# Filler matmuls on two 64-row halves of the array, one item apart, behind both score pairs of an odd step; the residual tile replaced in halves

## The chip, the cores and the metric

The kernel runs on one core of a Trainium2 chip. Its engines are TensorE (PE in the profile, its weight loads PEld), VectorE (DVE), ScalarE (ACT), GpSimd (POOL) and SyncE (SP), which issues the DMAs. The metric is the time of one launch on the device, in microseconds.

## The reference

One transformer layer on x of 16 batches x 1024 tokens x 256, in float32, with 16 heads of 16:

```python
q, k, v = (split_heads(x @ W.T + b) for W, b in ((Wq, bq), (Wk, bk), (Wv, bv)))
attn = softmax(einsum('hbnd,hbmd->hbnm', k, q) * (1 / 16), axis=-1)
out = merge_heads(einsum('hbnm,hbmd->hbnd', attn, v)) @ Wo.T + bo
x = layernorm(x + out)
h = silu(x @ w_gate.T / 127) * (x @ w_up.T / 127)      # 768 wide
x = layernorm(x + h @ w_down.T / 127)
```

## The kernel before

**Steps.** A batch is 64 steps: 4 groups of 4 heads, two halves of 512 tokens, 8 tiles of 128 (k in 0..63). In each step the function score does two pairs of heads, pair 0 and pair 1. A pair is two matmuls that lie on partitions 0 to 50 and 64 to 114, so on the two 64-row halves of the array, side by side. Their result goes to scores[pair], two banks of PSUM; ACT makes the exponentials from it (L608) into probs. There are only the two pairs of banks, so pair p of step k+1 waits until the exponential of pair p of step k is done (probs_ready). The function products multiplies probs with v for two steps at once, at every even step, for steps k-2 and k-1: 16 float32 matmuls, each on all 128 rows and 32 columns of the array, four side by side.

**Fillers.** Everything else that PE has to do is cut into items and put between the steps: of the next batch qk (8 items of 6 matmuls of 512 columns), norm (2) and v (4 items of 12 matmuls of 256 columns); of the batch before out (4 of 12), x1T (4 items of 4 float32 transposes of 128), gate and up (12 each, 4 matmuls of 512) and down (4 items of 24 matmuls of 256). Apart from norm they use all 128 rows and 128 columns. FULL_BLOCKS gives the items of the 32 visits, one at each odd step: qk, out and x1T in the first 10, one gate and one up in each of the next 12, v and down in the last 10. An item takes one of the three ring banks (RINGS = 3) and, at its start, waits on ring_free for the item three before it to be drained. The drain is DVE's (drain_item), for qk and gate with an ACT instruction ahead of it (hi L580, tanh L589).

**Order on the engines.** All engines run in program order. On PE an odd step is pair 0, pair 1, fillers; an even step is pair 0, pair 1, products of two steps. Plan gives the orders of DVE, ACT and POOL from due times that are written out by hand. In a middle batch (1 to 14) they are FULL_PLAN's. Batch 0 has only the items of the next batch, batch 15 only those of the one before.

**The residual.** x_res, 1 MB, holds the residual and later the result. At the end of a batch SP stores the result in two halves, waits for both, loads the whole of the next x (L447 and near), and POOL adds the bias to all of it in one instruction (add_bias, L530); out 0 is drained after that.

**Names in the prediction.** take and scale are DVE's take_segment and scale_segment, which bring the sums of a finished half group from PSUM and divide; xT is scale_x (x to two float16 parts in x16, L799 and L801); x1 and y are normalise (L822), which waits for POOL's rstd (L510).

Of the kernel before, what the change touches and what calls it, by code (L numbers as in the profile page):

```python
# [9 lines left out]
ALU = mybir.AluOpType  # L10
# [4 lines left out]
P = 128  # L15
BATCHES = 16
TOKENS = 1024
DIM = 256
# [44 lines left out]
STACK = ROWS + SHIFT_ROWS  # L63

# [9 lines left out]
        "gate": (4, 216), "up": (4, 216), "down": (24, 108)}  # L74
PRE, POST = ("qk", "norm", "v"), ("out", "x1T", "gate", "up", "down")
# [10 lines left out]
def evenly(items, steps):  # L86
# [4 lines left out]
    for kind, j in items:  # L91
# [3 lines left out]
        for m in sorted(set(where)):  # L95
# [3 lines left out]
FULL_BLOCKS = (evenly(some("qk", 0, 1, 2, 3) + some("out", 0, 1, 2, 3)  # L99
                      + [item for j in range(4) for item in some("x1T", j) + some("qk", 4 + j)], 20)  # L100
               + [some("norm", *{3: (0,), 5: (1,)}.get(g, ())) + gate_up(g) for g in range(2 * HCHUNKS)]
               + evenly(some("v", 0, 1) + some("down", 0) + some("v", 2, 3) + some("down", 1, 2, 3), 20))
FULL = list(dict.fromkeys((kind, j) for block in FULL_BLOCKS for kind, j, *_ in block))

# [9 lines left out]
ONLY_POST = [item for item in FULL if item[0] in POST]  # L114
# [4 lines left out]
def base(b):  # L119

    return len(FIRST) if isinstance(b, int) and b == 0 else len(FIRST) + len(ONLY_PRE) + len(FULL) * (b - 1)


PREPARE = 8
XMAX, SCALE = 6, 22
POOL_XMAX, POOL_NORMS = 12.2, 48.9
# [66 lines left out]

PREPARES = [PER_GROUP * g + PREPARE for g in range(GROUPS - 1)] + [STEPS - 6]
FULL_PLAN, PRE_PLAN, POST_PLAN = Plan(FULL_BLOCKS, PREPARES), Plan(evenly(ONLY_PRE, PRE_STEPS), PREPARES), Plan(POST_BLOCKS, PREPARES[:-1])
# [7 lines left out]
def build(nc, x, xt, Wq_t, bq, Wk_t, bk, Wv_t, bv, Wo_t, bo, gate_t, up_t, down_t, out):  # L203
    ctx = ExitStack()
    with ctx:  # L205
# [113 lines left out]
        x_pre_loaded, x_res_loaded, x_res_biased = sem("x_pre_loaded"), sem("x_res_loaded"), sem("x_res_biased")  # L319
        ring_fill, ring_free = sem("ring_fill"), sem("ring_free")  # L320
# [20 lines left out]
        def _(sp):  # L341
# [32 lines left out]
            def store_result(b):  # L374
                for s in range(2):

                    sp.wait_ge(y_ready, 4 * b + 2 * (s + 1))
                    sp.dma_start(out_v[b][:, TPH * s:TPH * (s + 1), :], x_res[:, TPH * s:TPH * (s + 1), :]
                                 ).then_inc(out_stored, 16)


# [14 lines left out]
            def batch(b, first, last, ahead=2):  # L396
                if first:
                    load_stack(b, 1)
# [4 lines left out]
                if not first:  # L403
                    sp.wait_ge(scores_ready, UNITS * b)
                    load_stack(b, 1)
# [895 lines left out]
```

## Time and profile before

| | us |
|---|---|
| median of 3 runs | 2544.46 |
| lowest, highest | 2544.41, 2547.49 |
| span of the profiled execution | 2544.0 |
| PE busy in it | 2470.4 (97%) |
| ACT busy in it | 2132.0 (84%) |
| DVE busy in it | 1399.0 (55%) |
| POOL busy in it | 539.6 (21%) |

The busy time of PE is not that of a full array: the ends of matmuls are modelled, and a row with four matmuls of a pair of heads counts from the first start to the last end. What the array does is read from the starts: the time from the start of one group of matmuls to the start of the next.

### The profile page before, as it was taken

The numbers are of one execution on the slowest core, as the hardware profiler recorded it, in microseconds if no ns is written. First come the engines' busy times: TensorE is split into PE (matmuls) and PEld (weight loads), VectorE is DVE, ScalarE is ACT, GpSimd is POOL, SyncE is SP. The second block draws the span as 40 slices with busy tenths as digits, with TensorE's granted clock in tenths as the row PEclk, the third lists the DMA queues.
The fourth block names the chain that finished last, engine by engine and source line by source line (L and its number), as shares of the span: only waits on it lengthen the run. The fifth ranks groups of instructions, "written<-read, shape, count | busy, mean of one in ns | idle before, by whom it ended". The sixth has DMA issues, their size and how long they took to land. (4 is left out here: it accounts for less than half of the span.)

```text
span 2544.0 us, 48910 instructions
## 1 busy us (share of the span) xinstructions
PE 2470.4 (97%) x18062; PEld 884.2 (35%) x18062; DVE 1399.0 (55%) x3008; ACT 2132.0 (84%) x2370; POOL 539.6 (21%) x542
## 2 busy tenths in 40 slices
PE   4999999999999999999999999999999999999996
PEld 2223343433324333343433324333343433333333
DVE  5334556464654655556564654646465565654547
ACT  1997888888888888888888888888889888898881
POOL 2102222131221212222131221212222131221113
PEclk8999999999999999999999999999999999999998
DMA  4112021030212103021021202103121120212000
GB/s 145 50 49 79 28 88 43 23 101 27 91 33 75 59 17 109 23 85 43 31 93 27 93 31 81 55 15 109 27 81 43 37 87 26 93 31 60 27 22 29
DMA packets 81750, 144.20 MB, mean 57 GB/s; under 512 B 27584, under 2 KB 29504, under 8 KB 79424
## 3 DMA queue, kind: packets, MB, share of 16 engines
q1 hardware_dynamic: 79968, 139.81, 17.4%
q8 instruction: 178, 2.92, 0.5%
q14 instruction: 100, 0.82, 0.1%
q10 hardware_dynamic: 1504, 0.66, 0.1%
HBM read 88.48 MB, written 50.33 MB: 55 GB/s over the span
## 5 line engine op out<-in xcount | busy, mean ns | idle before, releaser
L608 ACT ACTIVATE probs<-psum 128x1024 f32<-128x1024 f32 x2048 | 1984.8, 1024 | 312.5 <-PE psum L1045 311.8
L1045 PE MATMUL psum<-probs,v 128*32 128x512 f32 x8192 | 995.7, 600 | 0.9 <-DVE flipped L877 0.4
L1045 PE MATMUL psum<-kstack,qstack 51*128 51x512 f16 x4096 | 637.5, 383 | 18.7 <-ACT probs L608 10.4
L1045 PEld LDWEIGHTS psum<-kstack,qstack 51*128 51x128 f16 x4096 | 150.5, 93 | 679.9 <-ACT probs L608 596.5
L1045 PEld LDWEIGHTS psum<-probs,v 128*32 128x32 f32 x8192 | 211.2, 109 | 470.3 <-issue 468.1
L517 POOL TENSOR_TENSOR ffn<-h,ffn 128x512 f16<-128x512 f32 x192 | 222.0, 1156 | 675.8 <-DVE ffn L793 675.8
L747 DVE SCALAR_TENSOR_TENSOR tanh_out<-tanh_out,psum 128x512 f32<-128x512 f32 x192 | 131.6, 686 | 287.2 <-ACT tanh_out L589 287.2
L510 POOL TENSOR_TENSOR rstd<-vareps,minus_half 128x2 f32<-128x2 f32 x128 | 91.1, 712 | 720.9 <-DVE vareps L815 720.8
L738 DVE SCALAR_TENSOR_TENSOR parts<-psum,scales,parts 128x512 f16<-128x512 f32 x128 | 95.3, 745 | 199.5 <-ACT parts L580 199.4
L1045 PE MATMUL psum<-ffn,gateT 128*128 128x512 f16 x768 | 199.8, 383 | 0.3 <-DVE ffn L781 0.3
L1045 PE MATMUL psum<-ffn,upT 128*128 128x512 f16 x768 | 198.0, 380 | 0.4
L1045 PE MATMUL psum<-downT,ffn 128*128 128x256 bf16 x1536 | 188.5, 273 | 0.0
L877 DVE STREAM_TRANSPOSE flipped<-psum 128x512 f32<-128x512 f32 x128 | 91.6, 716 | 170.3 <-PE psum L1045 170.3
L496 POOL TENSOR_TENSOR squares<-parts 128x512 bf16<-128x512 f16 x128 | 130.9, 1046 | 225.2 <-DVE parts L738 167.3
L1045 PEld LDWEIGHTS psum<-downT,ffn 128*128 128x128 f16 x1536 | 141.5, 98 | 59.6 <-issue 44.3
L789 DVE SCALAR_TENSOR_TENSOR h<-tanh_out,h_scale,psum 128x512 f32<-128x512 f32 x192 | 143.5, 747 | 18.7 <-DVE tanh_out L747 0.5
L589 ACT ACTIVATE tanh_out<-psum 128x512 f32<-128x512 f32 x192 | 116.3, 606 | 42.3 <-PE psum L1045 42.3
L822 DVE TENSOR_SCALAR x_res<-x_res,meanvar,rstd 128x256 f32<-128x256 f32 x256 | 93.4, 407 | 67.0 <-POOL rstd L510 67.0
L773 DVE SCALAR_TENSOR_TENSOR x_res<-psum,down_scale,x_res 128x512 f32<-128x512 f32 x64 | 47.9, 749 | 138.9 <-PE psum L1045 138.9
L580 ACT ACTIVATE parts<-psum,scales 128x512 f16<-128x512 f32 x128 | 88.9, 696 | 31.8 <-PE psum L1045 24.3
L530 POOL TENSOR_TENSOR x_res<-x_res,bo_all 128x2048 f32<-128x2048 f32 x16 | 72.6, 4540 | 169.5 <-DMA x_res<-in_L_attn_x 169.5
L1045 PEld LDWEIGHTS psum<-ffn,upT 128*128 128x128 bf16 x768 | 74.6, 98 | 93.9 <-DVE tanh_out L747 4.9
(120 smaller groups left out, 1617.0 us busy)
## 6 DMA issues: line engine op xcount, KB each, us to landing
parts_dram<-parts SPq DMA_DIRECT2D x64, 512.0 KB, 2.9
qstack<-parts_dram SPq DMA_DIRECT2D x384, 64.0 KB, 2.1
kstack<-parts_dram SPq DMA_DIRECT2D x384, 64.0 KB, 2.2
x_pre<-in_x_t SPq DMA_DIRECT2D x17, 1024.0 KB, 7.3
x_res<-in_L_attn_x SPq DMA_DIRECT2D x16, 1024.0 KB, 4.8
out<-x_res SPq DMA_DIRECT2D x32, 512.0 KB, 2.7
kstack<-shift_parts SPq DMA_DIRECT2D x384, 4.0 KB, 1.7
ffn<-in_L_ffn_w_gate SPq DMA_DIRECT2D x1, 768.0 KB, 7.1
```

The source lines that it names most:

```text
L496: nc.gpsimd.tensor_tensor(squares[:, idx, cols], parts[:, idx % 2, 0, cols], parts[:, idx % 2, 0, cols], ALU.mult).then_inc(squares_ready, 1)
L510: nc.gpsimd.tensor_tensor(rstd[:, tiles], vareps[:, tiles], minus_half[:, tiles], ALU.pow).then_inc(rstd_ready, 1)
L517: nc.gpsimd.tensor_tensor(hT[hf][1][:, hc, :], h32[:, g % 2, :], hT[hf][0][:, hc, :], ALU.subtract).then_inc(h_lo_ready, 1)
L580: nc.scalar.activation(parts[:, idx % 2, 0, hf * HALF:(hf + 1) * HALF], bank[RING + (start + n) % RINGS], ACT.Identity, bias=scales[:, par ...
L589: nc.scalar.activation(tanh_out[:, g % 2, :], bank[RING + (start + n) % RINGS], ACT.Tanh, scale=0.5 * W_SCALE).then_inc(tanh_ready, 1)
L608: nc.scalar.activation(probs[:, (STEPS * b + k) % SLOTS, 2 * pr:2 * pr + 2, :], scores[pr], ACT.Exp, scale=score_scale[par]).then_inc(prob ...
L738: nc.vector.scalar_tensor_tensor(out=parts[:, idx % 2, 1, cols], in0=o, scalar=scale[:, BIAS + idx:BIAS + idx + 1], in1=parts[:, idx % 2, ...
L747: nc.vector.scalar_tensor_tensor(out=gated, in0=gated, scalar=1.0, in1=o, op0=ALU.add, op1=ALU.mult).then_inc(ring_free, 1)
L789: nc.vector.scalar_tensor_tensor(out=h32[:, j % 2, :], in0=tanh_out[:, j % 2, :], scalar=h_scale[:, 0:1], in1=o, op0=ALU.mult, op1=ALU.mul ...
L822: ins = nc.vector.tensor_scalar(x_res[:, t, :], x_res[:, t, :], meanvar[:, t, 0:1], rstd[:, t:t + 1], ALU.subtract, ALU.mult)
L877: nc.vector.transpose(flipped[:, hf, :], bank[ACC]).then_inc(acc_free, 1)
L1045: return nc.tensor.matmul(o, lhsT, rhs, start=start, stop=stop)
```

## The change

Fillers of the middle batches are done on half the rows. MAIN lists the items in order: out 0 to 3, qk 0 to 7, gate and up 0 to 11, tile 0 to 7 (down, cut to one token tile each), v 0 to 3. Each item is done twice over the same columns: first its matmuls on partitions 0 to 63 (LOW), and then those on 64 to 127 (HIGH) into the same bank. A slot holds the LOW matmuls of one item and the HIGH matmuls of the item before it, one by the other: 1 + 1 of 512 columns, or 2 + 2 of 256. The first HIGH matmul of an item waits on the new semaphore half_made for the end of the last LOW matmul of that item. out, qk, tile and v have 6 slots, gate and up 4. The last item (v 3) is carried: its HIGH half comes in the next batch. VISITS gives 242 slots to the 32 odd steps, all behind both pairs. x1T and norm are done whole, on all rows, as side items: at even steps 8, 10, 12, 14 and 26, 30, between the pairs and the products. A new class Rolled gives the orders of DVE, ACT and POOL. Since v 3 needs the old x16, xT is now done at the start of the next batch, behind v 3 and ahead of the drain of out 0; the search for the maximum of x starts at step 9 in place of 6. x_res is stored, loaded and given its bias in two halves, each with its own semaphore.

```diff
+LOW, HIGH = slice(0, ROW_TILE), slice(ROW_TILE, P)
+MAIN = (some("out", 0, 1, 2, 3) + some("qk", *range(8)) + gate_up(*range(2 * HCHUNKS)) + some("tile", *range(TILES))
+        + some("v", 0, 1, 2, 3))
+CARRY = MAIN[-1]
+WIDTH = {"out": 6, "qk": 6, "gate": 4, "up": 4, "tile": 6, "v": 6}
+VISITS = [(0, count, 0) for count in (
+    8, 8, 8, 6, 6, 6, 6, 9, 9, 10, 6, 10, 6, 10, 6, 10, 8, 8, 8, 8, 8, 8, 7, 7, 8, 6, 8, 7, 7, 8, 6, 6)]
+SIDES = {3: ("x1T", 0), 4: ("x1T", 1), 5: ("x1T", 2), 6: ("x1T", 3), 12: ("norm", 0), 14: ("norm", 1)}
-XMAX, SCALE = 6, 22
-POOL_XMAX, POOL_NORMS = 12.2, 48.9
+XMAX, SCALE = 9, 22
+POOL_XMAX, POOL_NORMS = 14.2, 48.9
...
+class Rolled(Plan):
+    def __init__(self, prepares, carried, carries):
+        slots = []
+        for phase in range(len(MAIN) + (not carries)):
+            low = phase if phase < len(MAIN) else None
+            high = phase - 1 if phase or carried else None
+            wide = [0 if n is None else WIDTH[MAIN[n][0]] for n in (low, high)]
+            slots += [(low if i < wide[0] else None, high if i < wide[1] else None, i) for i in range(max(wide))]
...
+        if carried:
+            last = carry_ready
+            dve = [(last, "v", CARRY[1], -1)] + [(last + 0.3 + 1.5 * hf, "xT", hf, 0) for hf in range(HALVES)]
...
+            def replace_half(b, s):
+                store_half(b, s)
+                sp.wait_ge(out_stored, 32 * b + 16 * (s + 1))
+                sp.dma_start(x_res[:, TPH * s:TPH * (s + 1), :], x_v[1:BATCHES][b][:, TPH * s:TPH * (s + 1), :]
+                             ).then_inc(x_res_loaded[s], 16)
...
-                    store_result(b - 1)
-
-                    sp.wait_ge(out_stored, 32 * b)
-                    sp.dma_start(x_res[:, :, :], x_v[1:BATCHES][b - 1]).then_inc(x_res_loaded, 16)
+                    replace_half(b - 1, 0)
+                    load_shift(b + 1, 0)
+                    replace_half(b - 1, 1)
...
+            def half_waits(plan, kind, j, n, start, pre, post):
+                pe.wait_ge(ring_free, start + n - RINGS + 1)
...
+            def slot(plan, b, low, high, i, w_parts):
+                todo = []
+                for rows, which in ((LOW, low), (HIGH, high)):
+                    if which is not None:
+                        kind, j = MAIN[which]
+                        each = COST[kind][0] // WIDTH[kind]
+                        todo += [(m / each, rows, which, kind, j, each * i + m) for m in range(each)]
+                for _, rows, which, kind, j, m in sorted(todo, key=lambda entry: entry[0]):
+                    n = plan.number(which)
+                    if m == 0 and rows is LOW:
+                        half_waits(plan, kind, j, n, base(b), b + 1, b - 1)
+                    elif m == 0:
+                        pe.wait_ge(half_made, len(MAIN) * (b - 1) + which + 1)
+                    ins = half_mm(kind, j, m, rows, bank[RING + (base(b) + n) % RINGS], w_parts)
+                    if m == COST[kind][0] - 1:
+                        ins.then_inc(half_made if rows is LOW else ring_fill, 1)
...
+            def full(b, par, w_parts):
+                plan = plan_of(b)
+                for k in range(STEPS):
...
+                    here = plan.segments[(k - 1) // 2] if k else ((), (), ())
+                    score(b, k, False, (0,))
...
+                    for low, high, i in here[0 if k % 2 else 2]:
+                        slot(plan, b, low, high, i, w_parts)
+                    score(b, k, False, (1,))
+                    if k % 2:
+                        for low, high, i in here[1]:
+                            slot(plan, b, low, high, i, w_parts)
+                        continue
+                    if k and k // 2 - 1 in SIDES:
+                        n = plan.place(*SIDES[k // 2 - 1])
+                        do_item(plan, n, 0, COST[plan.items[n][0]][0], base(b), b + 1, b - 1, w_parts)
+                    for earlier in (k - 2, k - 1):
...
             def everything(w_parts):
                 for b in range(1, BATCHES - 1, 2):
-                    batch(b, 1, False, False, w_parts)
-                    batch(b + 1, 0, False, False, w_parts)
+                    full(b, 1, w_parts)
+                    full(b + 1, 0, w_parts)
```

## Rows read from the trace of the kernel before

**Rows 1.** The page's first part: busy time of each engine, its share and instructions.

```profile
PE 2470.4 (97%) x18062; PEld 884.2 (35%) x18062; DVE 1399.0 (55%) x3008; ACT 2132.0 (84%) x2370; POOL 539.6 (21%) x542
```

**Rows 2.** One middle batch: its length, busy time (count) PE, PEld, DVE, ACT, POOL; clock.

```profile
1265.48:1417.52 152.04, 152.04 (x1129) 54.94 (x1129) 85.44 (x184) 133.12 (x149) 33.20 (x33) 1.00 0.18 57
```

**Rows 3.** Timeline of PE (start, us, engine, line, operation, count), gate and up visit.

```profile
1202.51 0.61 PE L1045 MATMUL psum<-kstack,qstack 51*128 51x512 f16 x4
1203.05 1.04 PE L1045 MATMUL psum<-ffn,gateT 128*128 128x512 f16 x4
1203.92 1.03 PE L1045 MATMUL psum<-ffn,upT 128*128 128x512 f16 x4
1204.88 0.61 PE L1045 MATMUL psum<-kstack,qstack 51*128 51x512 f16 x4
1205.42 1.92 PE L1045 MATMUL psum<-probs,v 128*32 128x512 f32 x16
```

**Rows 4.** Timeline of all engines, the same visit: ACT, tanh and two exponentials.

```profile
1204.77 0.60 ACT L589 ACTIVATE tanh_out<-psum 128x512 f32<-128x512 f32 x1
1205.31 1.94 ACT L608 ACTIVATE probs<-psum 128x1024 f32<-128x1024 f32 x2
```

**Rows 5.** Timeline of all engines, PE in a short visit of 14 down matmuls.

```profile
1263.31 0.61 PE L1045 MATMUL psum<-kstack,qstack 51*128 51x512 f16 x4
1263.84 1.70 PE L1045 MATMUL psum<-downT,ffn 128*128 128x256 bf16 x14
1265.48 0.64 PE L1045 MATMUL psum<-kstack,qstack 51*128 51x512 f16 x4
1266.05 1.92 PE L1045 MATMUL psum<-probs,v 128*32 128x512 f32 x16
1267.91 0.61 PE L1045 MATMUL psum<-kstack,qstack 51*128 51x512 f16 x4
```

**Rows 6.** Timeline of PE: an x1T item ahead of qk, a norm ahead of gate.

```profile
1297.08 0.66 PE L1048 MATMUL psum<-ident,x_res 128*128 128x128 f32 x4
1297.57 1.46 PE L1045 MATMUL psum<-x,Wq 128*128 128x512 f16 x6
...
1330.62 0.40 PE L1045 MATMUL psum<-squares,heads 128*32 128x512 bf16 x4
1330.95 1.04 PE L1045 MATMUL psum<-ffn,gateT 128*128 128x512 f16 x4
```

**Rows 7.** Timeline of DVE: scale, the drain of out, x1, x1T, xT.

```profile
1270.00 0.25 DVE L885 RECIPROCAL inv<-flipped 128x16 f32<-128x16 f32 x1
...
1272.12 0.69 DVE L896 TENSOR_TENSOR out<-flipped,out 128x512 f16<-128x512 f32 x1
...
1290.83 0.74 DVE L768 SCALAR_TENSOR_TENSOR x_res<-psum,out_scale,x_res 128x512 f32<-128x512 f32 x1
...
1293.79 0.74 DVE L822 TENSOR_SCALAR x_res<-x_res,meanvar,rstd 128x256 f32<-128x256 f32 x2 [0.80 <-POOL rstd L510]
...
1302.61 0.68 DVE L779 CAST ffn<-psum 128x512 f16<-128x512 f32 x1
1303.37 0.69 DVE L781 TENSOR_TENSOR ffn<-psum,ffn 128x512 f16<-128x512 f32 x1
...
1397.07 0.75 DVE L799 TENSOR_SCALAR x<-x_pre,scales 128x1024 f16<-128x1024 f32 x1
1397.89 1.28 DVE L801 SCALAR_TENSOR_TENSOR x<-x_pre,scales,x 128x1024 f16<-128x1024 f32 x1
```

**Rows 8.** Timeline of ACT: hi of a qk item, behind the exponentials.

```profile
1274.92 0.70 ACT L580 ACTIVATE parts<-psum,scales 128x512 f16<-128x512 f32 x1
```

**Rows 9.** Timeline of POOL: the bias added to all of x_res.

```profile
1277.31 4.54 POOL L530 TENSOR_TENSOR x_res<-x_res,bo_all 128x2048 f32<-128x2048 f32 x1 [8.79 <-DMA x_res<-in_L_attn_x]
```

**Rows 10.** The page's DMA issues: count, KB of one, us from issue to landing.

```profile
x_res<-in_L_attn_x SPq DMA_DIRECT2D x16, 1024.0 KB, 4.8
out<-x_res SPq DMA_DIRECT2D x32, 512.0 KB, 2.7
```

More of the change, by code:

```diff
@@ L73 @@
 COST = {"x1T": (4, 109), "qk": (6, 216), "norm": (1, 330), "v": (12, 108), "out": (12, 108),
-        "gate": (4, 216), "up": (4, 216), "down": (24, 108)}
-PRE, POST = ("qk", "norm", "v"), ("out", "x1T", "gate", "up", "down")
+        "gate": (4, 216), "up": (4, 216), "down": (24, 108), "tile": (12, 108)}
 def some(kind, *js):
@@ L113 @@
                + [half for j in range(4) for half in halves("down", j)])
-ONLY_POST = [item for item in FULL if item[0] in POST]
+ONLY_POST = (some("out", 0, 1, 2, 3) + some("x1T", 0, 1, 2, 3) + gate_up(*range(2 * HCHUNKS)) + some("down", 0, 1, 2, 3))
 FIRST = some("qk", *range(QK)) + some("v", 0) + some("norm", 0, 1) + some("v", 1, 2, 3)
@@ L396, in batch @@
             def batch(b, first, last, ahead=2):
-                if first:
-                    load_stack(b, 1)
+                if not first:
+                    sp.wait_ge(scores_ready, UNITS * b)
+                load_stack(b, 1)
                 if not last:
@@ L451, in _ @@
             batch(BATCHES - 1, False, True)
-            store_result(BATCHES - 1)
+            for s in range(2):
+                store_half(BATCHES - 1, s)
             sp.wait_ge(out_stored, 32 * BATCHES)
@@ L592, in batch @@
             def batch(b, par, first, last):
[L593 removed]
+                plan = plan_of(b, first, last)
                 def extras(k, h):
@@ L775, in drain_item @@
                     find_stats(j)
+                elif kind == "tile":
+                    nc.vector.scalar_tensor_tensor(out=x_res[:, j, :], in0=o[:, 0:DIM], scalar=down_scale[:, 0:1],
+                                                   in1=x_res[:, j, :], op0=ALU.mult, op1=ALU.add).then_inc(ring_free, 1)
+                    if j % 2:
+                        find_stats(j // 2)
                 elif kind == "x1T":
@@ L899, in batch @@
             def batch(b, par, first, last):
-                plan = PRE_PLAN if first else POST_PLAN if last else FULL_PLAN
+                plan = plan_of(b, first, last)
                 def once(k):
@@ L1146, in do_item @@
                     ins.then_inc(ring_fill, 1)
+            def half_waits(plan, kind, j, n, start, pre, post):
+                pe.wait_ge(ring_free, start + n - RINGS + 1)
+                if kind == "qk" and j < 2:
+                    pe.wait_ge(x_scaled, 2 * pre + j + 1)
+                elif kind == "out" and j % 2 == 0:
+                    pe.wait_ge(out_ready, 4 * post + 3 + j // 2)
+                elif kind == "gate":
+                    if j == 0 and post == 0:
+                        pe.wait_ge(ffn_weights_ready, 1)
+                    if j % HCHUNKS == 0:
+                        pe.wait_ge(ring_free, start + plan.place("x1T", 2 * (j // HCHUNKS) + 1) + 1)
+                elif kind == "tile" and j % TPH == 0:
+                    pe.wait_ge(h_lo_ready, 2 * HCHUNKS * post + HCHUNKS * (j // TPH + 1))
```

178 lines of the change are left out of this document (143 added, 35 removed).

## The prediction

> **What bounds the kernel now.** First the page's busy times: PE 97%, ACT 84%, DVE 55% [rows 1]; the reader is to see that only PE and ACT can be the bound. Then the length of one middle batch by stretch: 152.04 us at full clock, ACT busy 133 of them [rows 2]. There are 14 such batches, 2129 of the 2544.0 us; only they are changed much. Then the timeline of PE. A visit with gate and up, from pair 0 of an odd step: 0.54 us to the fillers, 1.83 to the next pair, 0.54 to the products [rows 3], 1.86 to the pair after them [rows 5], in sum 4.77. Nothing waits in it. One round of 512 columns takes 0.216 (gate to up 0.87 for four, 0.01 of it for the first) [rows 3]. So two rounds of scores leave 0.11 of the 0.54, and eight filler rounds leave 0.10 of the 1.83: **about 0.10 is lost each time the array goes from one tiling to another**, four times per visit.
>
> But ACT is close behind. In a short visit (14 x 0.109 us of fillers), PE's second pair row lasts 0.64 in place of 0.61: it waits for ACT [rows 5]. From the odd step's pair 0 to the products 2.74 pass, and with the products (1.86) the visit takes 4.60 [rows 5]. The 2.74 is a chain, not PE's work: 0.43 from pair 0 to its exponential, 1.94 for two exponentials [rows 4], 0.05 back, 0.31 from pair 1 to the products. Since the products stand behind pair 1 of the even step, which needs the odd step's second exponential, **no visit can be shorter than 4.60**, however few fillers it has.
>
> **The change, part by part.**
>
> *Two tiling changes fewer.* Scores and fillers are now both on 64-row halves. A visit of c slots then takes on PE 0.44 (two pairs) + 0.216c + 0.54 + 1.86. With c = 8 that is 4.57, so the floor of 4.60 holds: 0.17 less than 4.77, not the 0.20 removed. With 9 it is 4.78, with 10 5.00, with 6 or 7 the floor, 4.60. The Trainium skill, "TensorEngine Tiling (Array Packing)", section Tiling Modes, says that changing the mode drains the array; the 0.10 of rows 3 is that, and no more than that is to be won.
>
> *Half matmuls.* The rows of the scores show two halves side by side: four matmuls of 512 columns in 0.43 [rows 3]. So I take a slot at 0.216, whole items' price; 242 slots against 240 before, since two boundaries between items of 4 and of 6 slots leave a half idle. Twice the weight loads are at no cost if they run side by side as the scores' do.
>
> *The new wait.* At the first HIGH matmul of an item PE waits for the end of the LOW half of the same item, which it issued one round earlier. Behind it in PE's queue stands everything, first the next LOW matmul. No row shows PE waiting for itself. The nearest: ACT starts 0.43 after the start of the pair that it reads [rows 4]. A round of 0.216 lies between, so HIGH starts 0.21 behind LOW. It keeps that lag, and pair 0 of the even step, with ACT and the products behind it, comes as much later. A second boundary in the same visit costs nothing more, as HIGH's own lane is by then as late. Bounds: 0 if the wait is answered at once (nothing can be gained by it), 0.27 if PE is as slow as after other engines. I take 0.20. It falls in the 25 visits with a boundary behind their first slot; the other seven (visits 3 to 6, 25, 30, 31, counted from 0) have 6 slots. So c = 8 gives 4.77, 9 gives 4.98, 10 gives 5.20; in a visit of 7 (2.69 to the products against 2.74) or 6 the floor hides it.
>
> *Sum over the visits.* VISITS has 8 twelve times, 9 twice, 10 four times, 7 four times, 6 ten times: 12 x 4.77 + 2 x 4.98 + 4 x 5.20 + 14 x 4.60 = 152.4.
>
> *Side items.* An x1T took 0.49 inside the fillers [rows 6]. Between pair 1 and the products it adds a tiling change, 0.59, in a visit of 6 that already waits for ACT in its odd step; the two do not overlap, since x1T stands behind the wait. Four: 2.4. A norm has the tiling of the products: 0.22 for one round, in place of 0.33 [rows 6]; two: 0.4. Together 2.8.
>
> *hi and tanh.* They stand behind the odd step's second exponential. One of 0.6 (tanh [rows 4]) or 0.7 (hi [rows 8]) just fits into ACT's pause of the even step; two in one visit (visit 8, visit 10) don't, and pair 1 of the next odd step waits some 0.5. I take 1.0 in all.
>
> *xT at the head of the batch.* DVE's queue there, from when the last products of the batch before are done, 2.5 us in: take 0.6, scale 2.8 and a pause to 6.1, v 3 to 6.7, xT twice 2.1 to 10.9, out 0 with its statistics 2.1 (from its start to x1's, less the pause of 0.80), 0.8 for POOL's rstd, x1 0.65, out 1 and out 2 to 18.6 (out 2's bank free at 17.3), x1 twice, out 3 to 22.2, x1T 0 1.45 to 23.6 [rows 7]. PE comes to qk 0 (odd step 7) at 3 x 4.77 + 2.8 = 17.1 and waits 0.2 for out 2's bank; to qk 1 (step 9) at 22.3 and waits 1.4 for x1T 0's, of which 0.45 would have been spent on ACT anyway. Net 1.2. Unhidden it was 0 before, as xT lay in a stretch where DVE waited. Bounds 0.3 and 3; I take 1.0.
>
> *Ring.* A bank is now held for two phases, so gate g+1 waits for the drain of up g-1 one phase earlier. In an 8-slot visit this falls together with the lag above; in three of the 10-slot visits it may add 0.2 each. Taken at nothing, 0.6 in the range.
>
> *Residual in halves, and SP.* The whole bias took 4.54 and began 12 us into the batch [rows 9]. Now y 3 is due at step 60, so about 10 us before the batch's end; store and load (2.7 and at most 4.8 [rows 10]) and a half's bias of 2.3 end near its start, and out 0 is drained 10.9 in. Cost 0. On SP the halves' waits stand ahead of the next stack and shift loads; these are due at the next batch's step 0 (shift, moved ahead of the second half) and step 16, so several us off: 0. If that cover failed, PE would wait once per batch for about one load of 2 to 5.
>
> *Total.* 152.4 + 2.8 + 1.0 + 1.0 = 157.2 per batch against 152.04: +5.1, times 14 is +71. Against the profiled execution's 2544.0 (the median of the runs is 0.5 more): **2615**.
>
> **Rivals.**
>
> *The wait is answered at once* (no lag; for it: nothing in the trace shows the wait). Then 12 x 4.60 + 2 x 4.78 + 4 x 5.00 + 14 x 4.60 = 149.2, with the same 4.8 behind it 154.0: +2.0 a batch, 2572.
>
> *Faster: PE's own work sets the time.* The mechanism is that ACT's chain shifts against PE's from visit to visit, so that short visits are not held at the floor and the 10,6,10,6 pattern averages out. With no lag, a batch is 32 x 2.84 + 242 x 0.216 + 2.8 = 146.0, plus 1 to 2 for DVE: -4.5 to -5, 2480. It decides where a visit of 6 slots takes under 4.5. Against it: the 4.60 of rows 5. For it: PE's 97% [rows 1]. A mixture of this and the last (some lag, some averaging) gives about 2544, no change.
>
> *PE is short of instructions.* Half matmuls double the filler instructions; of 256 columns they come at one per 54 ns, with a weight load each. The fastest fillers now are one matmul and one load per 0.109 [rows 5]. If that were the limit, the 96 slots of out, tile and v would take 0.44: up to +20 a batch; if a tenth of that, 2645. The Trainium skill, "TensorE: Matmul & The Clock Gate", section "Wait — 56ns, not 53.3ns?", gives about 62 ns per matmul where the sequencer decodes them in software; by that such a slot is estimated at 0.25 and the sum at some 40 us more, in place of nothing. No row here shows a rate above one per 0.109 kept up.
>
> *The halves don't run side by side.* A slot would cost 0.43, over 3200. The scores speak against it.
>
> **How the numbers follow.** Forecast 0.46; answered at once 0.16; PE alone, faster 0.25; mixture, no change 0.07; short of instructions 0.05; halves one after the other 0.01. Its own range: lag 0.15 to 0.27 and DVE 0.3 to 3 give 2585 to 2660. The range reaches down into the faster case: 2495 to 2665. Faster by over 0.2% (what a measurement can tell) 0.25, within 0.2% 0.07, slower 0.68.
>
> **What would show it.** In the profile after: pair to fillers 0.43 to 0.45 and fillers to pair without the 0.10 (step one). HIGH's first matmul of an item 0.2 behind LOW's, and the even step's pairs late by as much (the lag). Visits of 6 slots at 4.60, with x1T at 5.2, visits of 10 at 5.2 (the floor). PE waiting on DVE at steps 7 and 9, DVE without a pause from 3 to 24 us in. The prediction is wrong if 6-slot visits are shorter than 4.5, if 8-slot gate visits take 4.6, or if slots of 256 columns take more than 0.22.

## The result and the profile after

| | before | after |
|---|---|---|
| median of the runs, us | 2544.43 (4 runs: 2542.72 to 2547.49) | 2797.73 (4 runs: 2789.18 to 2799.03) |
| ratio, 95% interval | | 1.0987 [1.097, 1.1005] |
| span of the profiled execution, us | 2544.0 | 2786.8 |
| mean granted clock of PE in it | 0.990 | 0.973 |

The kernel became 253 us slower; the forecast was 71 slower. Parts 1 and 2 of the page of the changed kernel: busy time of each engine, and PE's busy tenths and granted clock in 40 slices.

```profile
PE 2539.2 (91%) x22766; PEld 947.6 (34%) x22766; DVE 1442.5 (52%) x3060; ACT 2142.5 (77%) x2370; POOL 546.1 (20%) x558
...
PE   4988998989999898998989989899899998989997
...
PEclk9999999999999999999999999999999999999998
```

Against [rows 1], every engine's share fell, PE's from 97% to 91%, although PE's busy time rose by 69 us. So PE stands still, and not for want of an engine with more work: the new time is waiting. The table of waits of the changed kernel says for what (waiting engine and line, releaser: us in total, times, longest):

```profile
PEld psum L1160 <- ACT probs L715: 599.7, 801, 3.1
...
PEld psum L1160 <- DVE h L901: 154.7, 165, 3.9
...
PE psum L1160 <- DVE h L901: 97.0, 56, 3.4
...
PEld psum L1160 <- PE psum L1160: 87.9, 305, 0.3
...
ACT parts L687 <- DMA parts_dram<-parts: 45.3, 15, 7.5
```

The first line, the waits of the scores for the exponentials, is what it was before (598.7). L901 is DVE's drain of an up item, and behind it is 3.9 us at the longest. In the kernel before, the same pair of lines stands at 0.4:

```profile
PEld psum L1045 <- DVE h L789: 12.1, 39, 0.4
```

Next, where in a batch the time is lost. The table gives the length of each visit (from the start of the first products matmul of an even step to that of the next; median over the 14 middle batches), worked out from the starts of PE's matmuls. "Foreseen" is the prediction's own figure for that visit. Visits that are not shown agree with it within 0.03.

| visit: odd step | slots | before | foreseen | after |
|---|---|---|---|---|
| 0 to 2: 1, 3, 5 | 8 | 4.76 | 4.77 | 4.80 |
| 3, 4: 7, 9 | 6, x1T | 4.78 | 5.19 + the DVE wait | 6.16, 6.20 |
| 5, 6: 11, 13 | 6, x1T | 4.78, 4.81 | 5.19 | 5.19 |
| 7, 8: 15, 17 | 9 | 4.81 | 4.98 | 5.00 |
| 9: 19 | 10 | 4.81 | 5.20 | 5.41 |
| 10: 21 | 6 | 4.76 | 4.60 | 6.18 |
| 11: 23 | 10 | 4.76 | 5.20 | 5.74 |
| 12: 25 | 6, norm | 4.76 | 4.82 | 9.39 |
| 13: 27 | 10 | 5.09 | 5.20 | 6.35 |
| 14: 29 | 6, norm | 4.76 | 4.82 | 5.40 |
| 15: 31 | 10 | 5.09 | 5.20 | 5.20 |
| 16: 33 | 8 | 4.76 | 4.77 | 8.14 |
| 17: 35 | 8 | 4.76 | 4.77 | 5.43 |
| 20: 41 | 8 | 4.76 | 4.77 | 5.24 |
| 24, 26, 29: 49, 53, 59 | 8 | 4.60 | 4.77 | 4.80 |
| 25, 30, 31: 51, 61, 63 | 6 | 4.60 to 4.67 | 4.60 | 4.60 |

A mean middle batch takes 170.1 us against 152.2, so 14 of them are 251 of the 253. Of the 12.9 above the foreseen 157.2, visits 12 to 20 hold 10.8, of which 7.9 are in two visits, at steps 25 and 33. The rest is 1.6 at step 21 and 1.0 at steps 7 and 9 (2.0 above their 5.19, of which 1.0 was foreseen).

The timeline of PE and DVE at step 25 of one middle batch of the changed kernel (start, us, engine, line, operation; in brackets the idle time before it and its releaser):

```profile
1280.42 0.61 PE L1160 MATMUL psum<-kstack,qstack 51*128 51x512 f16 x4
1280.56 0.72 DVE L989 STREAM_TRANSPOSE flipped<-psum 128x512 f32<-128x512 f32 x1 [1.26 <-PE psum L1160]
...
1280.87 0.38 PE L1160 MATMUL psum<-ffn,gateT 64*128 64x512 f16 x1
...
1280.87 0.38 PE L1160 MATMUL psum<-ffn,upT 64*128 64x512 f16 x1
...
1281.09 0.37 PE L1160 MATMUL psum<-ffn,upT 64*128 64x512 f16 x1
...
1281.70 0.43 DVE L999 TENSOR_TENSOR scaled<-flipped,inv 128x256 f32<-128x256 f32 x1
1282.20 0.71 DVE L1004 STREAM_TRANSPOSE flipped<-scaled 128x512 f32<-128x512 f32 x1
...
1283.49 0.69 DVE L1008 TENSOR_TENSOR out<-flipped,out 128x512 f16<-128x512 f32 x1
1284.10 0.74 DVE L901 SCALAR_TENSOR_TENSOR h<-tanh_out,h_scale,psum 128x512 f32<-128x512 f32 x1
...
1284.89 0.39 PE L1160 MATMUL psum<-ffn,upT 64*128 64x512 f16 x1 [3.43 <-DVE h L901]
```

Two slots into the visit, the LOW half of up 2 wants its bank. That is the bank of up 1, whose HIGH half ended in the slot just before, at 1281.09 plus a round. Its drain L901 is ready to run, but DVE does take and scale first (from L989 at 1280.56 to L1008, done at 1284.1), since that is the order written out for it. PE starts again 0.79 after the start of the drain, 3.80 after the start of its last matmul. ACT needs no more of this time than the two exponentials of the visit, and the next scores stand behind the fillers, so nothing makes up for it.

This order came with the change. In the kernel before, up 1 is finished in the visit of step 23, and its drain stands ahead of take and scale; in the changed kernel up 1 is finished two slots into step 25, and Rolled puts it behind them. The timeline of DVE in the kernel before, at the same place of a batch (the drain of up 1, the first instruction of take, the last of scale):

```profile
1172.20 0.75 DVE L789 SCALAR_TENSOR_TENSOR h<-tanh_out,h_scale,psum 128x512 f32<-128x512 f32 x1
...
1173.41 0.72 DVE L877 STREAM_TRANSPOSE flipped<-psum 128x512 f32<-128x512 f32 x1
...
1176.53 0.69 DVE L896 TENSOR_TENSOR out<-flipped,out 128x512 f16<-128x512 f32 x1
```

The granted clock after it, in the table of stretches of the changed kernel (length, busy time (count) of PE, PEld, DVE, ACT and POOL, clock, DMA share, GB/s): from the pairs of step 24 to those of step 26, with the stall in it, and from there to the pairs of step 28, in batch 6 and then in batch 7.

```profile
1106.37:1114.97 8.60, 5.17 (x40) 1.50 (x36) 5.22 (x11) 4.29 (x5) 2.31 (x2) 0.86 0.03 6
1114.97:1122.46 7.49, 7.49 (x50) 2.13 (x48) 2.53 (x4) 4.56 (x6) 0.01 (x1) 0.71 0.00 0
1277.98:1285.77 7.79, 4.36 (x40) 1.31 (x37) 5.21 (x11) 4.28 (x5) 1.50 (x2) 1.00 0.03 5
1285.77:1291.13 5.36, 5.36 (x50) 1.92 (x48) 2.45 (x4) 4.56 (x6) 0.82 (x1) 1.00 0.01 3
```

The same 50 entries of PE take 7.49 in batch 6 and 5.36 in batch 7. In batch 6 the mean granted clock is 0.71, a mixture of the 2.4 GHz level and the 1.2 GHz one, and PE is busy all through; in batch 7 it is 1.00. PE stood still for 3.43 in the stretch ahead of it in both (8.60 less 5.17, 7.79 less 4.36). The Trainium skill, "TensorE: Matmul & The Clock Gate", section "Part 1: The HAM clock gate", says that the array's clock is halved according to how busy PE has lately been; the row of batch 6 agrees, at 2.1 us more, and that of batch 7 shows that such a stall does not always bring it. Batches 5 and 7 have a granted clock of 1.00 from end to end. In them the visits at steps 25 and 33 take 7.95 and 7.30 against the medians of 9.39 and 8.14, and the visits at steps 25 to 41 lie 6.8 above what was foreseen, where the mean of all 14 batches is 10.2. So of the 10.8, 6.8 is waiting and some 4 the half clock behind it.

### The profile page after: what moved, and what is told of

Read it like the earlier page. It is cut to its first block and busy times, and to the rows that moved or that the text cites. A ratio compares the mean times of both kernels' runs of the same rounds, so it can differ in the third digit from the quotient of the medians.

```text
span 2786.8 us, 58468 instructions
## 1 busy us (share of the span) xinstructions
PE 2539.2 (91%) x22766; PEld 947.6 (34%) x22766; DVE 1442.5 (52%) x3060; ACT 2142.5 (77%) x2370; POOL 546.1 (20%) x558
## 5 line engine op out<-in xcount | busy, mean ns | idle before, releaser
L1160 PE MATMUL psum<-kstack,qstack 51*128 51x512 f16 x4096 | 698.6, 387 | 67.7 <-ACT probs L715 57.4
L1160 PE MATMUL psum<-ffn,upT 64*128 64x512 f16 (+1 forms) x1440 | 385.6, 388 | 60.7 <-DVE h L901 60.2
L1160 PEld LDWEIGHTS psum<-kstack,qstack 51*128 51x128 f16 x4096 | 198.1, 95 | 685.1 <-ACT probs L715 584.4
L1160 PE MATMUL psum<-ffn,gateT 64*128 64x512 f16 (+1 forms) x1440 | 385.4, 389 | 37.0 <-DVE h L901 36.7
L901 DVE SCALAR_TENSOR_TENSOR h<-tanh_out,h_scale,psum 128x512 f32<-128x512 f32 x192 | 143.3, 746 | 312.2 <-PE psum L1160 309.9
L845 DVE SCALAR_TENSOR_TENSOR parts<-psum,scales,parts 128x512 f16<-128x512 f32 x128 | 94.5, 748 | 286.1 <-ACT parts L687 286.1
L1160 PE MATMUL psum<-downT,ffn 64*128 64x256 bf16 (+1 forms) x2880 | 226.7, 270 | 0.0
L989 DVE STREAM_TRANSPOSE flipped<-psum 128x512 f32<-128x512 f32 x128 | 90.6, 708 | 197.9 <-PE psum L1160 197.9
L1160 PEld LDWEIGHTS psum<-ffn,gateT 64*128 64x128 bf16 (+1 forms) x1440 | 119.1, 96 | 208.1 <-DVE h L901 76.6
L934 DVE TENSOR_SCALAR x_res<-x_res,meanvar,rstd 128x256 f32<-128x256 f32 x256 | 123.6, 524 | 120.5 <-POOL rstd L615 120.3
L1160 PEld LDWEIGHTS psum<-downT,ffn 64*128 64x128 f16 (+1 forms) x2880 | 162.7, 94 | 65.5 <-PE psum L1160 19.0
L1160 PE MATMUL psum<-x,Wq 64*128 64x512 f16 (+1 forms) x720 | 140.5, 381 | 35.8 <-DVE ffn L893 16.8
L1160 PEld LDWEIGHTS psum<-ffn,upT 64*128 64x128 bf16 (+1 forms) x1440 | 115.2, 96 | 118.4 <-DVE h L901 74.0
L687 ACT ACTIVATE parts<-psum,scales 128x512 f16<-128x512 f32 x128 | 87.2, 695 | 83.3 <-DMA parts_dram<-parts 45.3
```

Of the source, the lines that this page charges most:

```text
L687: nc.scalar.activation(parts[:, idx % 2, 0, hf * HALF:(hf + 1) * HALF], bank[RING + (start + n) % RINGS], ACT.Identity, bias=scales[:, par ...
L845: nc.vector.scalar_tensor_tensor(out=parts[:, idx % 2, 1, cols], in0=o, scalar=scale[:, BIAS + idx:BIAS + idx + 1], in1=parts[:, idx % 2, ...
L901: nc.vector.scalar_tensor_tensor(out=h32[:, j % 2, :], in0=tanh_out[:, j % 2, :], scalar=h_scale[:, 0:1], in1=o, op0=ALU.mult, op1=ALU.mul ...
L934: ins = nc.vector.tensor_scalar(x_res[:, t, :], x_res[:, t, :], meanvar[:, t, 0:1], rstd[:, t:t + 1], ALU.subtract, ALU.mult)
L989: nc.vector.transpose(flipped[:, hf, :], bank[ACC]).then_inc(acc_free, 1)
L1160: return nc.tensor.matmul(o, lhsT, rhs, start=start, stop=stop)
```

## The experiments

The theory after the result (A): two things meet. An item on two half arrays holds its bank for two phases, so the next user asks for it one phase after it was filled in place of two; behind a norm, which takes a number in the ring, it asks in the slot right behind (up 2 at step 25). And DVE's order puts the 2.8 us of scale ahead of the drain in three odd half groups (steps 25, 33, 41). The rival (B): the half matmuls, or their waits on one another, make the stalls, and DVE's line is only the last name in the list. Later a second pair: which of the two things is enough alone.

**e1: only DVE's order.** take and scale of those three half groups are due later, behind the drain of the up item.

```diff
-            dve += [(TILES * seg + 1.0, "take", seg - 1, 0), (TILES * seg + 1.4, "scale", seg - 1, 0)]
+            late = 0.49 if seg in (3, 4, 5) else 0.0
+            dve += [(TILES * seg + 1.0 + late, "take", seg - 1, 0), (TILES * seg + 1.4 + late, "scale", seg - 1, 0)]
```

> One edit to the changed kernel: in the gate stretch (segments before steps 24, 32 and 40) DVE's take and scale of the finished segment come behind the drain of up 1, up 5 and up 9, not ahead of it (due times 0.49 of a step later). Theory A (a bank is held for two phases, so the next LOW half needs the drain of an up that has just ended, and that drain stands behind 3.5 us of scale work in DVE's queue): the visit at step 25 falls from 7.8 to 8.6 us to about 5.7 (the bare drain of up 1, 1.0, is still waited for), the one at step 33 from 7.7 to 4.8, step 41 from 5.3 to 4.8, and the visits after them lose their half-clock part; some 9 us a batch, 125 in all: about 2670. Theory B (half matmuls, their loads or the lag cost the time): under 20 us less, above 2770.

Measured: 2696.05, ratio 1.060 [1.0581, 1.0619], clock 0.991. Steps 25 and 33 fell from 9.39 and 8.14 to 5.40 and 5.00, step 27 to 6.01; a batch takes 163.2. So 102 of the 253 us hang on the place of two operations in DVE's queue, those of the half clock included. It is 26 us above what was expected. Step 25 came out under the 5.7 foreseen, but part of the wait moved to the visits behind: in batches without the half clock steps 27 and 35 went from 5.20 and 4.80 to 6.01 and 5.52. Steps 33 and 41 take 5.00 in place of 4.8.

**e2: also the search for the maximum of x later on POOL.** In the changed kernel one line of ACT waits for a DMA, 15 times, 45.3 us in all and 7.5 at the longest. The timeline of DVE, POOL and ACT before step 21:

```profile
1250.38 0.75 DVE L845 SCALAR_TENSOR_TENSOR parts<-psum,scales,parts 128x512 f16<-128x512 f32 x1 [2.24 <-ACT parts L687]
...
1255.24 0.38 POOL L593 PARTITION_ALL_REDUCE xmax_all<-xmax_safe  x1 [6.82 <-issue]
...
1262.74 4.03 POOL L601 TENSOR_TENSOR squares<-parts 128x512 bf16<-128x512 f16 x4 [7.13 <-DVE parts L845]
...
1268.11 0.69 ACT L687 ACTIVATE parts<-psum,scales 128x512 f16<-128x512 f32 x1 [3.16 <-DMA parts_dram<-parts]
```

The all-reduce over the partitions shows 0.38 busy, but 6.82 us of POOL's queue go by ahead of it and another 7.13 behind it, before the squares. The profile puts the second gap on DVE's L845; but the parts that the first of these squares reads were written by 1251.13, over 11 us earlier, so it is not that wait. In e2, where the all-reduce stands elsewhere in POOL's queue, the same two gaps are 6.38 and 6.99, both put on "issue". The squares behind it come late, with them the store of parts, and with the store ACT's hi, which writes parts again; ACT's exponentials stand behind hi.

```diff
-POOL_XMAX, POOL_NORMS = 14.2, 48.9
+POOL_XMAX, POOL_NORMS = 17.2, 48.9
```

> The edit of e1_up_first, and POOL's all-reduce of the maximum of x comes behind the squares of qk 2 and qk 3 (POOL_XMAX 17.2 in place of 14.2), so that the second store of parts, for which ACT's hi of qk 6 waits, goes out earlier. Theory A2 (ACT's 3 us wait for that store holds back the exponentials at step 21): the visits at steps 21 and 23 fall from 5.9 and 6.2 to about 5.1 and 5.4, 20 us less than e1_up_first, about 2650. Rival (that wait is hidden, the visits are long by their 10 slots alone): no change from e1_up_first.

Measured: 2670.51, 1.050 [1.0481, 1.0519], 25.5 under e1 where 20 were expected. Step 21 fell from 6.21 to 4.60, the floor, and ACT's wait went from 15 times to once:

```profile
PEld psum L1161 <- DVE h L902: 76.5, 165, 1.4
...
ACT parts L688 <- DMA parts_dram<-parts: 7.6, 1, 7.6
```

The same rows show that 1.4 at the longest are still waited for the up drain (L902 here).

**d1 and d2: whole items in place of halves.** Both make an item whole (one matmul on all rows) in the slots in which its HIGH half was. The order of everything else stays. d1 still takes the bank a phase before, where the LOW half took it; d2 takes it when the item begins. The diff is the main part of d1's (do_item also gets a branch for whole tiles); d2 also drops the half_waits, since do_item has the same wait at its own first matmul.

```diff
                 for _, rows, which, kind, j, m in sorted(todo, key=lambda entry: entry[0]):
                     n = plan.number(which)
                     if m == 0 and rows is LOW:
                         half_waits(plan, kind, j, n, base(b), b + 1, b - 1)
-                    elif m == 0:
-                        pe.wait_ge(half_made, len(MAIN) * (b - 1) + which + 1)
-                    ins = half_mm(kind, j, m, rows, bank[RING + (base(b) + n) % RINGS], w_parts)
-                    if m == COST[kind][0] - 1:
-                        ins.then_inc(half_made if rows is LOW else ring_fill, 1)
+                    if rows is HIGH:
+                        do_item(plan, n, m, m + 1, base(b), b + 1, b - 1, w_parts)
```

> The changed kernel with whole matmuls: the LOW half issues only its waits (ring_free and the data), and the item is then done on all 128 rows where its HIGH half stood. Order of all engines, slots and the time for which a bank is held are those of the changed kernel; there is no half_made wait, no half matmul, and two tiling changes more in each visit. Theory A (order and banks are the cause): the long visits stay, other 8-slot visits go from 4.80 to 4.77, in all 2760 to 2810. Theory B (halves are the cause): under 2640.

> As d1_whole_early, but the waits stand where the whole item starts, so a bank is held for one phase. Theory A: against d1 each wait for a bank ends up to one phase (0.86 us of gate or up, 1.3 of qk) earlier: the stalls of 1.0 and 1.3 at steps 7 and 9 go, those of 3.8 and 2.8 at steps 25 and 33 become 2.9 and 1.9: 4 to 5 us a batch, some 60 less than d1, 2700 to 2750. If holding the bank matters little and only DVE's order does: within 20 of d1.

Measured: d1 2801.66, 1.101 [1.099, 1.103]; d2 2628.68, 1.034 [1.0322, 1.0359]. Waits for the up drain in d1:

```profile
PEld psum L1160 <- DVE h L901: 175.4, 165, 3.8
...
PE psum L1160 <- DVE h L901: 98.5, 56, 3.3
```

and in d2:

```profile
PEld psum L1160 <- DVE h L901: 3.2, 11, 0.4
```

d1 settles A against B: it has no half matmul and no half_made, has the changed kernel's waits for the up drain to the count (165 and 56), and takes as long. What the halves do to the time is in the moment at which they ask for the bank. d2 was 71 us under the lower end of what was expected. I had allowed for the stalls to become shorter by a phase of 4 slots, 0.9; but where a phase ends at a visit's end, a phase later is a visit later, so nothing of them was left (step 25 4.83, step 33 4.76).

**b1, b2, b3: the two causes put into the kernel before.** b1 puts take and scale ahead of the drain of up, b2 has each gate and up of the middle batches ask for its bank one item early (tight is true there), b3 does both.

```diff
+            ahead = blocks is FULL_BLOCKS and s in (3, 4, 5)
+            dve += [(TILES * s + (0.3 if ahead else 0.55), "take", s - 1, 0),
+                    (TILES * s + (0.4 if ahead else 1.3 if s else 2.7), "scale", s - 1, 0)]
...
-                    pe.wait_ge(ring_free, start + n - RINGS + 1)
+                    early = 2 if tight and kind in ("gate", "up") and n else 1
+                    pe.wait_ge(ring_free, start + n - RINGS + early)
```

> The kernel before with one edit, in its middle batches: DVE's take and scale of the segments that end at steps 24, 32 and 40 come ahead of the drains of up 1, up 5 and up 9. A bank is still held for one phase only. Theory A (late drains cost only where the bank is wanted at once): the drain of up 1 ends some 4 us into the fillers of step 25, its bank is wanted at step 27, so nothing waits: within 0.2% of 2544. Rival (DVE's order alone makes the stalls): three stalls of 1 to 3 us a batch, 2600 to 2650.

> The kernel before, with each gate and up of the middle batches waiting for one item more to be drained (the item two before it, not three), which is what holding a bank for two phases asks. DVE's order is that of before. Theory A: up g-1 is drained about 1.1 us after the end of its visit and wanted 3.9 after it: within 0.2% of 2544. Rival (two banks are too few in themselves): over 2600.

> Both edits on the kernel before. Theory A (only the two together cost): up 2, 0.9 us into the fillers of step 25, waits for up 1, whose drain ends 4.0 in behind take (0.7) and scale (2.8): 3.1 us, the same at step 33, 1.1 at step 41, 7.3 a batch, 102 in all, and a little for the clock behind them: 2645 to 2680. Rival (the stalls of the changed kernel need its halves or its slots): as b1 and b2, 2544.

| | us | ratio, 95% interval |
|---|---|---|
| b1, order | 2547.83 | 1.0018 [1.0009, 1.0028] |
| b2, bank | 2544.55 | 1.0005 [0.9995, 1.0014] |
| b3, both | 2697.51 | 1.0621 [1.0591, 1.065] |

Each alone costs next to nothing (b1 some 4 us, in the visit at step 27), both together 154 us. The timeline of b3, in a kernel with whole items only:

```profile
1070.15 1.04 PE L1047 MATMUL psum<-ffn,gateT 128*128 128x512 f16 x4
...
1070.88 0.42 DVE L889 TENSOR_TENSOR scaled<-flipped,inv 128x256 f32<-128x256 f32 x1
...
1073.28 0.74 DVE L791 SCALAR_TENSOR_TENSOR h<-tanh_out,h_scale,psum 128x512 f32<-128x512 f32 x1
...
1074.08 1.89 PE L1047 MATMUL psum<-ffn,upT 128*128 128x512 f16 x4 [2.89 <-DVE h L791]
```

It is the picture of the changed kernel: scaled, then the drain, and PE released by it 0.80 after its start. b3's visits at steps 25 and 33 take 9.08 and 9.11. It cost 18 us more than the top of what was expected. In batches 1, 2 and 4 the granted clock is 1.00 in the visit at step 25, and it takes 7.82 or 7.83, so 3.1 above the 4.76 of before, as foreseen; what lies above that goes with the half clock (0.969 in the mean). It shows in the rows above: the four matmuls of up take 1.89, those of gate before the stall 1.04. A stretch of it right behind the stall (columns as above):

```profile
1075.90:1081.64 5.74, 5.74 (x37) 1.40 (x37) 1.87 (x3) 4.21 (x5) 1.17 (x1) 0.87 0.03 4
```

**e3: HIGH one slot further behind LOW** from tile 1 on, against the wait of PE for itself. One slot of only HIGH is added in the last visit.

```diff
+            lows, highs = [(a, i) for a, _, i, _ in slots[head:]], [(c, i) for _, c, _, i in slots[head:]]
+            slots[head:] = [(a, c, i, m) for (a, i), (c, m) in zip(lows + [(None, 0)], [(None, 0)] + highs)]
```

> e2_up_xmax, and from tile 1 to v 3 each HIGH half starts one slot later (one slot without HIGH at the head of that stretch, one without LOW at its end, 243 slots), so that the LOW half for whose end it waits was issued two rounds earlier. Theory L (the 0.2 us by which an 8-slot visit exceeds 4.60 is PE's wait for its own LOW half): the 8-slot visits at steps 49, 53 and 59 fall by 0.2, the one at step 49 from 4.82 to about 4.60; visits of 6 and 7 slots stay, as ACT's chain holds them; 0.6 a batch, about 2662. Rival (the 0.2 is the price of running halves with 256 columns, or of twice the loads): step 49 stays at 4.8.

Measured: 2673.59, 1.0505 [1.0488, 1.0523], a batch 161.8 against e2's 161.5. The visits that the edit was for did what was expected: steps 49 and 59 went from 4.80 to 4.60. PE's timeline in such a visit of e2, and then of e3:

```profile
1293.68 0.61 PE L1161 MATMUL psum<-kstack,qstack 51*128 51x512 f16 x4
1294.13 2.14 PE L1161 MATMUL psum<-downT,ffn 64*128 64x256 bf16 x32
1296.00 0.70 PE L1161 MATMUL psum<-kstack,qstack 51*128 51x512 f16 x4
1296.63 0.64 PE L1161 MATMUL psum<-probs,v 128*32 128x512 f32 x4
```

```profile
1295.63 0.61 PE L1169 MATMUL psum<-kstack,qstack 51*128 51x512 f16 x4
1296.07 1.92 PE L1169 MATMUL psum<-downT,ffn 64*128 64x256 bf16 x32
1297.82 0.62 PE L1169 MATMUL psum<-kstack,qstack 51*128 51x512 f16 x4
1298.37 1.06 PE L1169 MATMUL psum<-probs,v 128*32 128x512 f32 x8
```

In both, pair to fillers is 0.45 and 0.44; fillers to the next pair is 1.87 with the wait and 1.75 without, and the products follow 0.63 and 0.55 behind it. The lag of one round is what a visit of 8 pays above the floor. It is lost again at step 7, which went from 6.10 to 6.57, and step 53 stayed at 4.79. The traces say where. At step 53 PE waits at its first filler for the bank of a tile, so for DVE again. At the head, POOL's bias of the second half of x_res starts 2.43 us behind the first products of the batch in e3 and 1.96 in e2 (medians of batches 2 to 14), and the DVE instruction that runs beside it lasts until it is done; step 7 grows by the same 0.47. The timeline of e3 at step 53 and, of the same batch, at its head, where a CAST of 0.43 takes 2.55:

```profile
1305.42 0.66 PEld L1169 LDWEIGHTS psum<-downT,ffn 64*128 64x128 f16 x14 [0.48 <-DVE x_res L893]
```

```profile
1173.11 2.37 POOL L646 TENSOR_TENSOR x_res<-x_res,bo_all 128x1024 f32<-128x1024 f32 x1 [9.97 <-DMA x_res<-in_L_attn_x]
1173.21 2.55 DVE L1015 CAST out<-flipped 128x512 f16<-128x512 f32 x1
```

**e4 and e5: even visits.** e4 takes the 10,6 pattern away (8 slots in all 13 visits from step 19 on), moves the norms to visits 13 and 17, and has scale (but not take) behind the drain; it keeps e2's place of the all-reduce and has 7 slots in place of 6 at steps 51 and 61. e5 is e4 with d2's whole items, asked for late.

```diff
-    8, 8, 8, 6, 6, 6, 6, 9, 9, 10, 6, 10, 6, 10, 6, 10, 8, 8, 8, 8, 8, 8, 7, 7, 8, 6, 8, 7, 7, 8, 6, 6)]
+    8, 8, 8, 6, 6, 6, 6, 9, 9, 8, 8, 8, 8, 8, 8, 8, 8, 8, 8, 8, 8, 8, 7, 7, 8, 7, 8, 7, 7, 8, 7, 6)]
-SIDES = {3: ("x1T", 0), 4: ("x1T", 1), 5: ("x1T", 2), 6: ("x1T", 3), 12: ("norm", 0), 14: ("norm", 1)}
+SIDES = {3: ("x1T", 0), 4: ("x1T", 1), 5: ("x1T", 2), 6: ("x1T", 3), 13: ("norm", 0), 17: ("norm", 1)}
```

> The changed kernel with POOL_XMAX 17.2, the slots spread evenly over the gate stretch (8 in each visit from step 19 on in place of 10 and 6 in turn, one gate and one up in each, 7 in place of 6 at steps 51 and 61), the norms at steps 28 and 36, away from the segments, and DVE's scale (not its take) behind up 1, up 5 and up 9. Theory F (a short visit costs 4.60 whatever it holds, so unequal visits lose what the long ones add; and a norm makes the next LOW half need an up that has just ended): the 13 visits from step 19 to 43 take 64 to 65 in place of 67.9 in e2_up_xmax, 3 less a batch, about 2630. Rival (time goes by the number of slots alone): no change from e2_up_xmax, 2670.

> e4_even with whole matmuls on 128 rows in place of the two halves, and the waits where the whole item starts (a bank is held for one phase, four tiling changes in a visit, no half_made). Theory A: what is left of the waits for banks goes (steps 7 and 9, and behind the norms, 3 to 4 us a batch), while 8-slot visits stay at 4.77: about 2580. Theory B (the halves' two tiling changes fewer are worth their 0.2 once the order is right): slower than e4_even.

Measured: e4 2665.76, 1.0481 [1.0464, 1.0499], so 5 us better than e2 where 40 were expected. Its 13 even visits sum to 66.7 against 67.7: the two with a norm take 6.58 each, the others 4.60 to 5.28. Outside them step 7 rose from 6.10 to 6.51 and step 53 from 4.80 to 5.22. A norm takes a number in the ring, and the item behind it is thereby set against a bank filled one item later; with halves that costs the wait for a drain in both places tried (in e4 PE stands for 1.54 at steps 27 and 35, released by L901). e5 came to 2582.78, 1.0154 [1.0137, 1.0171], as expected: there the same two visits take 4.99. Its wait for the up drain:

```profile
PEld psum L1160 <- DVE h L901: 3.2, 11, 0.4
```

So of the 121 us that e4 has above the kernel before, 83 go when the bank is asked for late and the halves (with their lag) are gone. The 38 that stay lie mostly in visits 3 to 9, at the head of the batch and in the x1T as side items: step 7 takes 5.93 in e5, steps 9 to 13 5.19, against 4.8 before. The kernel before remains the fastest of all that ran.

**e6: less xT at the head of the batch.** As e2, with the second xT instruction cut to 32 of its columns; this leaves out most of the low float16 part of x.

```diff
+                    nc.vector.scalar_tensor_tensor(out=x16[:, 1, 0, hf * HALF:hf * HALF + 32],
+                                                   in0=x_pre[:, 0, hf * HALF:hf * HALF + 32],
```

> e2_up_xmax with the second instruction of each xT cut from 1024 to 32 elements in the middle batches (the low part of x16 is left as it was but for 32 columns, so that the output is not the reference's): 2 x 1.2 us less in DVE's queue at the head of a batch, nothing else changed. Theory X (the stalls at steps 7 and 9 are DVE's queue with xT at its head): the visits at steps 7 and 9 (5.34 and 6.47) lose about 2.3 together, 30 us, about 2638. Rival (they wait for the banks' longer hold or for the residual's halves whatever DVE does first): within 8 of e2_up_xmax.

Measured: 2646.5, 1.0408 [1.039, 1.0425], 24 us under e2, where 30 were expected. Steps 7 and 9 went from 6.10 and 6.20 to 5.19 each, which is the foreseen price of a visit of 6 with an x1T and nothing else (the 5.34 and 6.47 of the expectation are not the medians of e2 for these visits); a batch went from 161.5 to 159.7. So DVE's queue at the head of the batch is what PE waits for there. At step 9 the early asking for the bank is needed too: with all of xT in place, but the bank asked for late, that visit takes 5.19 in d2 and e5, while step 7 stays at 5.60 and 5.93.

## Why the prediction was right or wrong

**The sign and the floor: right.** No visit of the middle batches got under 4.60 in the changed kernel. A visit of 6 slots takes 4.60 at steps 51, 61, 63, of 7 4.60, and step 21 came to 4.60 once ACT's wait was gone (e2). That is the ACT chain of [rows 4, 5], and it refutes the faster rival: visits of 6 do not average with those of 10.

**The lag: right.** PE's wait for itself took one round. The timeline of the changed kernel where HIGH of a qk item begins:

```profile
1264.52 0.38 PE L1160 MATMUL psum<-ffn,gateT 64*128 64x512 f16 x1
1264.73 0.09 PEld L1160 LDWEIGHTS psum<-x,Wk 64*128 64x128 f16 x1 [0.34 <-PE psum L1160]
...
1264.74 0.39 PE L1160 MATMUL psum<-x,Wk 64*128 64x512 f16 x1
...
1265.39 0.38 PE L1160 MATMUL psum<-x,Wk 64*128 64x512 f16 x1
1265.40 0.38 PE L1160 MATMUL psum<-kstack,qstack 51*128 51x512 f16 x1
```

HIGH (x, Wk) waits and then runs one round behind, and its last matmul starts as late as the scores of pair 0. The page's waits of PE for itself, 305 times at 0.3, are that. Visits of 8, 9 and 10 slots without another wait took 4.80, 5.00 and 5.20 against 4.77, 4.98 and 5.20; e3 removed it at steps 49 and 59 and got the 0.20 back. The rival that the wait is answered at once falls.

**Slots, side items, tiling changes, the residual on SP: right.** Two halves started within 10 ns of each other, and slots of 256 columns kept nearly the same price (the 8 tile slots of e3 above take 1.75, so 0.219 each): PE was not short of instructions, and the halves run side by side. The visits with an x1T took 5.19, as worked out. No wait of PE stands behind the residual's loads. The residual in halves was not tried alone, and its bias was not free (below).

**The ring: this step failed.** The prediction put it as: "gate g+1 waits for the drain of up g-1 one phase earlier. In an 8-slot visit this falls together with the lag above; in three of the 10-slot visits it may add 0.2 each. Taken at nothing, 0.6 in the range." It measured 10.8 a batch, some 150 us with the half clock behind it. The step priced the drain at its own length. It did not lay DVE's queue beside it, as it had done for the head of the batch, and so missed that the change itself turns the order round: ahead of the drain now stand take and scale, 3.5 us, of which it had read the rows of scale [rows 7]. Put there in the kernel before they cost 4 us in all (b1), since the bank is not yet wanted. It also did not count the norm as a user of a ring number. d1 against d2 shows that the early asking is needed for the loss, e1 that DVE's order is, and b3 that the two are enough. No run isolates the share of the half clock; the two batches without it put it at some 4 of the 10.8, and the mean clock was 0.973 with the stalls and 0.991 without (e1).

**The head of the batch: mis-sized.** Taken at 1.0 (bounds 0.3 and 3), it measured 1.0 at each of steps 7 and 9, 2.0 in all. For step 9 the prediction had a wait of 1.4, of which 0.45 hidden, so that part held. For step 7 it had 0.2. The queue was the right one (e6), but one term in it was not, and it is that of the residual in halves ("a half's bias of 2.3 end near its start [...] Cost 0"): while POOL adds the bias to the second half of x_res, a DVE instruction of scale takes 1.62 in place of the 0.43 that it takes at step 25 above. The timeline of the changed kernel:

```profile
1215.68 2.36 POOL L637 TENSOR_TENSOR x_res<-x_res,bo_all 128x1024 f32<-128x1024 f32 x1 [8.15 <-DMA x_res<-in_L_attn_x]
...
1216.70 1.62 DVE L999 TENSOR_TENSOR scaled<-flipped,inv 128x256 f32<-128x256 f32 x1
```

DVE's is done 0.28 after POOL's. How late POOL's starts differs from batch to batch, and step 7 follows it: it takes 5.92, 6.19 and 6.45 where the bias starts 1.84, 2.11 and 2.38 behind the first products. In the two batches of d2 in which it starts at 0.87 and 0.98, step 7 takes the 5.19 of a visit without a wait. The Trainium skill, "Perfetto Trace Analysis", section "Optimizing Scalar/DVE Operations", says that POOL's only port to SBUF is DVE's second pair and that a DVE operation on two ports holds it alone. The rows agree in that the two did not run side by side; that DVE can be the one who waits is what they add.

**A step that was missing: POOL's all-reduce.** The change moved the search for the maximum from 12.2 to 14.2, and the prediction did not follow what is queued behind it on POOL. It cost 1.6 at step 21 (e2). What showed it first was an ACT line with a DMA as its releaser.

**hi and tanh** were taken at 1.0; steps 19 and 23 have 0.2 and 0.5 more than their slots.

In sum: 157.2 was foreseen, of which the visits' own prices held within 0.03; 10.8 for the ring, 1.6 for ACT's wait and 1.0 for the head make 170.6, less 0.2 of hi and tanh 170.4, against a mean batch of 170.1 (medians of visits don't add up to it exactly). The prediction's own range was not quite the sum of its terms: with the lag in its 18 visits of 8 to 10 slots, DVE's bounds and the 0.6 of the ring it comes to some 2594 to 2670, not 2585 to 2660. The measured time lies far above either. Still open: what the residual in halves would cost alone, and why the same stall is followed by the half clock in one batch and not in another.

## What to carry to other kernels

When an edit makes a buffer's holder keep it longer, price the next user's wait by the whole in-order queue ahead of the drain, not by the drain: in that queue look for the longest thing that is harmless only while the buffer is free, and look whether the change itself has moved it ahead. A change that keeps a ring's size but asks for a bank a phase earlier has used up a bank. And to tell which of two conditions costs, put each and both into the kernel before; here each was worth under 0.2%, and both 6%.

## What was not expected of the hardware

- After one visit in which PE stood for 3.43 us, the granted clock of the next stretch was 0.71 in one batch (7.49 us) and 1.00 in another (5.36 us), for the same work.
- Shorter stalls were followed by it too: in batch 6 of the changed kernel PE stood for 2.34 us at step 33, and that visit took 8.15 in place of the 7.30 that it took in batch 7 with the same stall at a clock of 1.00.
- A DVE instruction of 0.43 us took 1.62 (in e3 another of 0.43 took 2.55) while POOL added into x_res.
- POOL's all-reduce over partitions shows 0.38 us busy, has 6.82 us in front of it that the profile puts on "issue", and another 7.13 us behind it before POOL's next instruction, whose input had been ready for over 11 us.
